# Graph network, last attention layer: normed rows gathered and multiplied by tile, exponentials ahead of the preceding step's normalization, heads mixed in one instruction

## The reference

```python
xt = jnp.matmul(x, weight).reshape(-1, heads, out_ch)
row, col = (edge_index[0], edge_index[1])
alpha_l = jnp.einsum('ehd,hd->eh', xt[row], attn_l)
alpha_r = jnp.einsum('ehd,hd->eh', xt[col], attn_r)
alpha = jax.nn.softmax(jax.nn.leaky_relu(alpha_l + alpha_r, 0.01), axis=1)
tmp = jnp.einsum('nh,nhd->nd', alpha[:n], xt[col[:n]])
out = jnp.broadcast_to(tmp[:, None, :], (n, heads, out_ch))
```

## Time and profile before

| | us |
|---|---|
| median of 3 runs | 3559.73 |
| lowest and highest run | 3539.03, 3561.72 |
| the profiled execution, its own time | 3567.03 |
| its span, first to last instruction | 3565.2 |
| TensorE busy (matmuls) | 2424.9 |
| VectorE busy | 2395.4 |
| ScalarE busy | 1352.5 |
| GpSimd busy | 1734.6 |

### The profile page before, as it was taken

The page is one execution under the profiler, slowest core; times in us unless marked ns, Lnnn a source line. Parts: engine busy times, 40 slices in busy tenths (PEclk is TensorE's granted clock), DMA queues, the critical chain, the costliest instruction groups (busy, mean ns, idle before and its releaser), DMA issues. The chain is left out here.

```text
span 3565.2 us, 41686 instructions
## 1 busy us (share of the span) xinstructions
PE 2424.9 (68%) x12339; PEld 1976.6 (55%) x12339; DVE 2395.4 (67%) x4693; ACT 1352.5 (38%) x2800; POOL 1734.6 (49%) x1269
## 2 busy tenths in 40 slices
PE   4668733454555543666621999879999999925998
PEld 3522213454444443444421897469888988923788
DVE  5979945777777778877886544344565566615788
ACT  2268833444444441000000435424434434423776
POOL 0257887776667667888888777730000000042000
PEclk9779865555555555888855999889999999966999
DMA  9993224665555656555533774146545645340355
GB/s 373 351 355 34 22 26 130 174 171 164 165 165 166 172 170 137 133 142 134 143 40 39 202 177 89 1 103 185 175 126 172 185 130 173 118 103 8 109 173 176
DMA packets 338453, 517.84 MB, mean 145 GB/s; under 512 B 145379, under 2 KB 227100, under 8 KB 331580
## 3 DMA queue, kind: packets, MB, share of 16 engines
q1 hardware_dynamic: 190254, 436.41, 38.2%
q0 software_dynamic: 134768, 58.41, 14.2%
q10 hardware_dynamic: 13214, 20.35, 1.7%
HBM read 369.65 MB, written 145.38 MB: 144 GB/s over the span
## 5 line engine op out<-in xcount | busy, mean ns | idle before, releaser
L1133 PE MATMUL banks<-rows_r,lhs_r 128*128 128x448 f32 x3500 | 899.1, 372 | 84.0 <-issue 41.6
L728 POOL DMA_INDIRECT counts<-wts x391 | 637.4, 1630 | 307.9 <-DMA counts<-ring 141.0
L1133 PEld LDWEIGHTS banks<-rows_r,lhs_r 128*128 128x128 f32 x3500 | 667.8, 191 | 152.9 <-issue 74.8
L741 POOL DMA_INDIRECT weights<-wts x391 | 620.9, 1588 | 161.8 <-issue 159.1
L1133 PE MATMUL banks<-ring_r,lhs_r 128*128 128x448 f32 x1750 | 525.8, 370 | 0.0
L749 POOL DMA_INDIRECT reg<-tab_p,w x416 | 406.9, 978 | 217.9 <-issue 122.8
L548 DVE SCALAR_TENSOR_TENSOR ring_r<-ring,dinv,rows_r 128x896 fp32r<-128x896 f32 (+1 forms) x300 | 303.7, 1033 | 309.5 <-ACT rows_r L535 309.3
L1221 PE MATMUL banks<-lhs_r,oT 128*128 x416 | 203.3, 489 | 429.8 <-issue 346.6
L535 ACT ACTIVATE rows_r<-ring,dinv 128x896 fp32r<-128x896 f32 (+1 forms) x300 | 285.0, 951 | 399.3 <-PE banks L1133 342.0
L799 POOL DMA_INDIRECT el<-tab_l,base_i x25 | 24.0, 958 | 796.8 <-DMA tab_l<-reg 789.5
L1221 PEld LDWEIGHTS banks<-lhs_r,oT 128*128 128x128 f32 x416 | 131.9, 317 | 447.3 <-issue 447.0
(11 more groups left out here) (269 smaller groups left out, 4104.6 us busy)
## 6 DMA issues: line engine op xcount, KB each, us to landing
ring<-weights SPq DMA_DIRECT2D x225, 448.0 KB
ring<-counts SPq DMA_DIRECT2D x150, 448.0 KB
zbuf<-reg SPq DMA_DIRECT2D x208, 256.0 KB
reg<-zbuf SPq DMA_DIRECT2D x52, 1024.0 KB
counts<-ring SPq DMA_DIRECT2D x25, 1568.0 KB, 16.4
weights<-ring SPq DMA_DIRECT2D x25, 1568.0 KB
ring<-weights SPq DMA_DIRECT2D x75, 224.0 KB
dr<-low_rows_d SPq DMA_DIRECT2D x52, 256.0 KB
```

Of the source, the lines that this page charges most:

```text
L728: pool.indirect_dma_start(counts, bass.IndirectOffsetOnAxis(ap=ix_c[:, k:k + 1], axis=0), vals_c[:, k:k + 1], None, compute_op=ALU.add).th ...
L741: pool.indirect_dma_start(weights, bass.IndirectOffsetOnAxis(ap=ix_w[:, k:k + 1], axis=0), vals_w[:, k:k + 1], None, compute_op=ALU.add).t ...
L1133: m = pe.matmul(bank[:, 0:BLK], lhs[part], rows[:, c:c + BLK], start=first, stop=last)
```

## The change

Four things are changed, all in the third layer and its mixing.

- tab_x holds the normed rows themselves (256 columns) and is stored from g_nat as soon as a step's five tiles are normed; tab_l is stored last. For it TensorE multiplies the transposed tiles by the 4 source columns alone, into one bank (stage "lg"), once all groups are transposed.
- GpSimd gathers the normed rows first (x_edge), and the small rows of step q behind the normed rows of step q+1.
- The product is done on the gathered rows, by tile, in each step: TensorE transposes a tile (stage "gx"), ScalarE copies it to one of two buffers (edge_T), TensorE multiplies by 260 columns (stage "xt"), ScalarE copies the result to xt_edge. ScalarE does this, and the exponential of the next step, right behind the square root of a step and ahead of the normed tiles of the step before it.
- The four heads are multiplied, and added to x_nat, in one instruction each.

The diff:

```diff
--- before.py
+++ after.py
@@ -132,6 +132,20 @@
     return unit_keys(gi, 0) + unit_keys(gi, 1)
 
 
+def rows_step(q):
+
+    ts = range(q * LG, (q + 1) * LG)
+    order = [(ts[0], "gx")]
+    for t in ts[1:]:
+        order += [(t, "gx"), (t - 1, "xt")]
+    return order + [(ts[-1], "xt")]
+
+
+def normed_groups(q):
+
+    return range(max(0, q - 3) * LG // 4, -(-NT // 4) if q == NSPLIT else max(0, q - 2) * LG // 4)
+
+
 def psum_plan():
 
     tg = [(j, g) for g in range(-(-NT // 4)) for j in range(JH)]
@@ -160,12 +174,12 @@
     for li in range(3):
         add(f"agg1{li}", dense, "V")
         add(f"cv{li}", pairs, "V")
-    for g in range(-(-NT // 4)):
-        add("gT2", [(j, g) for j in range(JH)], "A")
-        if g:
-            add("xt", [(t,) for t in range(4 * g - 4, 4 * g)], "A")
-    add("xt", [(t,) for t in range(NT - 1 - (NT - 1) % 4, NT)], "A")
-    add("gT3", tg, "A")
+    add("gT2", tg, "A")
+    add("lg", [(0,)], "A")
+    for q in range(NSPLIT + 1):
+        for t, stage in rows_step(q) if q < NSPLIT else ():
+            add(stage, [(t,)], "A")
+        add("gT3", [(j, g) for g in normed_groups(q) for j in range(JH)], "A")
     add("xj", pairs, "V")
     add("xi", [(j, b) for j in range(JH) for b in range(NB)], "A")
     add("a1", [(b,) for b in range(NB)], "A")
@@ -207,7 +221,7 @@
         zbuf = nc.dram_tensor("zbuf", (P, KS, H), F32).ap()
         cells = nc.dram_tensor("cells", (NCH, P), F32).ap()
         low_rows_d = nc.dram_tensor("low_rows_d", (KS, P), BF16).ap()
-        tab_x = nc.dram_tensor("tab_x", (NP, XE), F32).ap()
+        tab_x = nc.dram_tensor("tab_x", (NP, H), F32).ap()
         tab_l = nc.dram_tensor("tab_l", (NP, HEADS), F32).ap()
         counts_rows = counts[0:SPARE].rearrange("(r c) o -> r (c o)", c=LD)
         weights_rows = weights[0:SPARE].rearrange("(r c) o -> r (c o)", c=LD)
@@ -323,7 +337,7 @@
         supT, x0T, dinv_row = view(RD, JH, NP), view(RE, JH, NP), view(RF, DR)
 
         gT2 = view(RF, JH, NP)
-        xt_nat, xt_edge = view(RD, NT, XW), view(RD + NT * XW, NT, XE)
+        x_edge, lg_nat, xt_edge = view(RD, NT, H), view(RD + NT * H, NT, HEADS), view(RD + NT * XW, NT, XE)
         mix = view(RD, NT, H)
 
         xiT, xj_nat, a1row = view(RD, JH, NP), view(RE, NT, H), view(RF, LD)
@@ -352,6 +366,7 @@
         out_pair = [w2a_flat[:, BLK:BLK + 2 * H].rearrange("p (t c) -> p t c", c=H), w2b[:, 2:4, :]]
         attn = w1[:, 0:2, :]
         attn_tmp = w1[:, 2:4, :]
+        edge_T = [attn_tmp[:, k, :] for k in range(2)]
         ab2row, wa2row = w2b[:, 0, :], w2b[:, 1, :]
 
         def table(k):
@@ -682,11 +697,11 @@
                     sp.dma_start(attn[:, 1, :], attn_r.rearrange("h d -> (h d)").unsqueeze(0).to_broadcast([P, H])).then_inc(gat_loaded, 16)
 
             for s in range(NSPLIT):
-                sp.wait_ge(drained_a, nth[number["xt", ((s + 1) * LG - 1,)]])
-                if s == NSPLIT - 1:
-                    sp.dma_start(tab_l.rearrange("(t p) c -> p t c", p=P), xt_nat[:, :, XE:XW]).then_inc(l_stored, 16)
+                sp.wait_ge(ln_out, 2 * NT + (s + 1) * LG)
                 sp.dma_start(tab_x[s * LG * P:(s + 1) * LG * P].rearrange("(t p) c -> p t c", p=P),
-                             xt_nat[:, s * LG:(s + 1) * LG, 0:XE]).then_inc(xt_stored, 16)
+                             g_nat[:, s * LG:(s + 1) * LG, :]).then_inc(xt_stored, 16)
+            sp.wait_ge(drained_a, nth[number["lg", (0,)]])
+            sp.dma_start(tab_l.rearrange("(t p) c -> p t c", p=P), lg_nat).then_inc(l_stored, 16)
             sp.wait_ge(filled, number["h3", (JH - 1, NB - 1)] + 1)
             sp.dma_start(ab2row, ab2.unsqueeze(0).to_broadcast([P, H])).then_inc(gat_loaded, 16)
             sp.dma_start(wa2row, wa2.unsqueeze(0).to_broadcast([P, H])).then_inc(gat_loaded, 16)
@@ -793,16 +808,16 @@
                 pool.dma_start(ix[:, 0:NT - 1], dram[0:full].rearrange("(t p) -> p t", p=P)).then_inc(gi_ready, 16)
                 pool.dma_start(ix[0:LAST, NT - 1:NT], dram[full:N].unsqueeze(1)).then_inc(gi_ready, 16)
             pool.wait_ge(gi_ready, 64)
-            pool.wait_ge(l_stored, 16)
-            for s in range(NSPLIT):
-                for t in range(s * LG, (s + 1) * LG):
+            pool.wait_ge(xt_stored, 16 * NSPLIT)
+            for s in range(NSPLIT + 1):
+                for t in range(s * LG, (s + 1) * LG) if s < NSPLIT else ():
+                    pool.indirect_dma_start(x_edge[:, t, :], None, tab_x,
+                                            bass.IndirectOffsetOnAxis(ap=i_dst[:, t:t + 1], axis=0)).then_inc(edge_x[s], 16)
+                if s == 1:
+                    pool.wait_ge(l_stored, 16)
+                for t in range((s - 1) * LG, s * LG) if s else ():
                     pool.indirect_dma_start(el[:, t, :], None, tab_l,
-                                            bass.IndirectOffsetOnAxis(ap=i_src[:, t:t + 1], axis=0)).then_inc(edge_l[s], 16)
-                if s == 0:
-                    pool.wait_ge(xt_stored, 16 * NSPLIT)
-                for t in range(s * LG, (s + 1) * LG):
-                    pool.indirect_dma_start(xt_edge[:, t, :], None, tab_x,
-                                            bass.IndirectOffsetOnAxis(ap=i_dst[:, t:t + 1], axis=0)).then_inc(edge_x[s], 16)
+                                            bass.IndirectOffsetOnAxis(ap=i_src[:, t:t + 1], axis=0)).then_inc(edge_l[s - 1], 16)
 
             pool.wait_ge(ln_out, 4 * NT)
             pool.tensor_tensor(x_nat, x_nat, g_nat, ALU.add).then_inc(x_plus, 1)
@@ -833,29 +848,30 @@
                         for j in range(JH):
                             bank = empty_bank(act, number[stage, (j, g)])
                             emptied(act.activation(dest[:, j, ts[0] * P:(ts[-1] + 1) * P], bank[:, 0:len(ts) * P], ACT.Copy))
-                        if stage == "gT2" and g:
-                            copy_rows(g - 1)
                     copied[0] = upto
 
                 if stage == "hT":
                     act.wait_ge(drained_v, 3)
+                before(0)
                 for q in range(NT // LG):
-                    before(q)
                     act.wait_ge(ln_var, k * (NT // LG) + q + 1)
                     ts = slice(q * LG, (q + 1) * LG)
                     act.activation(sc[:, 1, ts], sc[:, 0, ts], ACT.Sqrt).then_inc(ln_std, 1)
+                    if q + 1 < NT // LG:
+                        before(q + 1)
                     if q:
                         apply(q - 1)
                 apply(NT // LG - 1)
                 if stage:
                     copy_groups(-(-NT // 4))
-                if stage == "gT2":
-                    copy_rows(-(-NT // 4) - 1)
-
-            def copy_rows(g):
-                for t in tiles_of((g,), 4):
-                    bank = empty_bank(act, number["xt", (t,)])
-                    emptied(act.activation(xt_nat[:, t, :], bank[:, 0:XW], ACT.Copy))
+
+            def copy_rows(q):
+                for t, stage in rows_step(q):
+                    bank = empty_bank(act, number[stage, (t,)])
+                    if stage == "gx":
+                        emptied(act.activation(edge_T[t % 2], bank[:, 0:H], ACT.Copy))
+                    else:
+                        emptied(act.activation(xt_edge[:, t, :], bank[:, 0:XE], ACT.Copy))
 
             def copy_pairs(stage, dest):
                 for g in range(-(-NT // 2)):
@@ -994,7 +1010,11 @@
 
             layernorm(2, stage="gT2", dest=gT2)
 
+            bank = empty_bank(act, number["lg", (0,)])
+            emptied(act.activation(lg_nat.rearrange("p t c -> p (t c)"), bank[:, 0:NT * HEADS], ACT.Copy))
+
             def exponentials(q):
+                copy_rows(q)
                 act.wait_ge(exp_in, q + 1)
                 ts = slice(q * LG, (q + 1) * LG)
                 act.activation(al[:, ts, :], al[:, ts, :], ACT.Exp).then_inc(exp_out, 1)
@@ -1040,9 +1060,9 @@
                     pe.wait_ge(drained[plan[prev_of[g]][2]], nth[prev_of[g]])
                 return ps[bank_of[g]]
 
-            def to_T(stage, src_nat, done, base, behind=None):
-
-                for gi in range(-(-NT // 4)):
+            def to_T(stage, src_nat, done, base, groups=range(-(-NT // 4))):
+
+                for gi in groups:
                     for j in range(JH):
                         bank = open_bank(number[stage, (j, gi)])
                         ts = tiles_of((gi,), 4)
@@ -1052,10 +1072,6 @@
                             m = pe.transpose(bank[:, (t - ts[0]) * P:(t - ts[0] + 1) * P],
                                              src_nat[:, t, j * P:(j + 1) * P], ident[:, :])
                         m.then_inc(filled, 1)
-                    if behind and gi:
-                        behind(gi - 1)
-                if behind:
-                    behind(gi)
 
             def node_rows(stage, lhs, rhs, width=H, per=2, nk=JH, base=0, block_ready=None):
 
@@ -1305,20 +1321,34 @@
 
             pe.wait_ge(gat_w_ready, 2 * JH)
 
-            def row_group(g):
-
```

(52 more changed lines are left out.)

## The result

The changed kernel takes 3573.42 us (median of 13 runs, 3561.93 to 3581.79) against 3558.73 us for the kernel before (13 runs, 3539.03 to 3566.52). The ratio is **1.0050, 95% interval 1.0033 to 1.0066**: half a per cent slower, 14.7 us by the medians, where no change (-0.3 us) was forecast. The profiled execution of after is its fastest, 3561.93 us with a span of 3560.2; that of before was 8 us above its median. The two spans therefore hide the loss, and the stretch from the third normalization's first square root (3103.29 before, 3092.61 after: 10.7 us earlier, in work that the change leaves alone) to x@W2 is the thing to compare.

A forecast was written before the change was run, and what follows sets the result against it. Bound mostly by TensorE in line 1133's dense products; the change shifts only x@W2's start. Start -6.5, steps +1.2, tail -4.0, waits +9 sum to -0.3 us: forecast 3559 us, range 3534 to 3583.

The forecast's parts named there:

- The start: Third layer's tables: small table ready when before, five gathers instead of ten ahead of first logits, 6.5 us saved.
- the row's price: TensorE's new row of 50 four-column matmuls, 100 records: 17.5 us at 1.2 GHz, 8.8 at 2.4, taken as 13.
- The steps of the loop: Four mixing steps between logits: 18.35 us each without waits, 73.4 against 72.2 before, +1.2 us.
- R: Per-step block of ScalarE copies, TensorE transposes and products ahead of next logits: 8.8 us; 6.1 warm, 11.1 cold throughout.
- the tail: Last logits to x@W2: 3.6 us less waiting for the exponential and 0.4 from merged heads, -4.0 us.
- rival (b): Copies of gathered rows serialize the loop at 1.2 GHz, R 11.1: +22.4 us, 3582 us; chance 0.17.
- rival (c): Mixing loop: products hidden and loop paced by gathers, 12.9 us a step: -31 us, 3528 us; chance 0.06.
- rival (a): Mixing loop: TensorE stays at 2.4 GHz, R 6.1, no waits, fast small matmuls: -24.3 us, 3535 us; chance 0.17.
- Merged heads: VectorE's mixing: one 1,280-column instruction of about 1.48 us replaces four taking 1.70; 0.2 saved twice, 0.4 a step.
- The waits: Mixing loop while gathers run: before holds 23.3 us of waits; the new loop's share taken as 9, ends 0 and 18.
- The two rules: VectorE-GpSimd port lock and hidden instruction fetch: waits term 2 to 4 us instead of 9; sum some 4 us lower.
- Rival (d): Small table ready 8 us late since stores, ring loads and row gathers share DMA engines: 3567 us; chance 0.15.

The follow-up runs named there:

- k11: Changed kernel with the row of small matmuls 16 columns wide instead of 4; executed once, the row took 21.49 us against 21.47.
- k1: Changed kernel with the small table's 4-column product made group by group behind the transposes; ratio to the kernel before 1.0023 (1.0007 to 1.0040).
- k15: The kernel before, unchanged, run again on a chip where it takes 3454 to 3461 us; ratio 1.0004 (0.9994 to 1.0014).
- k7: The kernel before with VectorE's mixing held until all fifty gathers have landed; one run, 3596.64 us.
- k10: The changed kernel with TensorE's work on gathered rows held until all fifty gathers have landed; one run, 3614.28 us.
- k4: The kernel before with only the four heads multiplied, and added to x_nat, in one instruction each; ratio 0.9965 (0.9949 to 0.9980).
- k13: The kernel before with the four heads multiplied in one instruction, the addition left in four; ratio 1.0006 (0.9994 to 1.0019).
- k14: The kernel before with the addition to x_nat's four heads in one instruction, the multiplication left in four; ratio 1.0005 (0.9995 to 1.0016).
- k17: The kernel before with exponentials ahead and merged heads, on a chip where before takes 3454 to 3461 us; ratio 0.9993 (0.9983 to 1.0003).
- k6: The kernel before with only exponentials ahead and merged heads, products left ahead of the tables; ratio 0.9947 (0.9932 to 0.9963), repeated 0.9952.
- k16: The changed kernel, run again on a chip where before takes 3454 to 3461 us; ratio to before 1.0048 (1.0032 to 1.0065).

## Why the prediction was wrong

**The start: the step that failed outright.** "So 17.5 us at 1.2 GHz and, halved, 8.8 us at 2.4 ... I take 13": the row took 21.47 us, above even the upper bound. The small table was stored 7.9 us later than before instead of at the same time, and the start became +2.1 us instead of -6.5. The rest of this term was right: the row began 27.1 us behind the square root, as forecast within half a us, and five gathers fewer saved 6.2 us, forecast 6.5.

Two errors lie in the row's price. The nearest row was chosen by columns (50 against 4), though k11 shows no difference between 4 and 16: each record of such a row waits for a weight load of 128x128. The price of that load stood among the rows, as eight loads in 1.66 us, 0.21 each, and was used only for transposes; times 100 it gives 20.8. The row that was chosen says the same once its loads are read. The 0.175 us run from the start of its first matmul to the start of the next line's; its four weight loads began at 860.90 and the next line's at 861.75, 0.21 us each. And the clock: TensorE never rose in this row, although it was busy through all of it, while it did rise in the products' block. This window of after shows it:

```profile
3120.40:3142.00 21.60, 21.60 (x102) 21.28 (x101) 0.00 (x0) 0.56 (x2) 9.68 (x10) 0.50 0.47 61
```

The Trainium skill, "TensorE: Matmul & The Clock Gate", section "LDWEIGHTS (loading the stationary operand)", gives a load's time as its columns divided by 1.2 in ns, 107 ns for 128. k1's 0.122 us at 2.4 GHz is near it, the 0.213 at 1.2 GHz twice as long; an estimate from that figure puts the row at 10.7 us, half of what it took.

In before TensorE went from transposes to products and back without a gap, and its granted clock was 1.00 from 3105 to 3142. In after it only transposed there, with gaps; the clock fell from 1.00 to 0.50 between 3111 and 3112, 8 us ahead of the row. In k1, with small groups between the transposes, it fell between 3116 and 3117. That the products which were taken away had kept it up is likely, but no run tests it alone.

**The steps of the loop held.** R was put at 8.8 and measured 8.0, a step at 18.35 and measured 17.1 to 17.2, the tail at -4.0 and measured -4.2. The clock rises inside each block, as argued from the earlier trace rows. Four steps were thus put 5.0 us too high (73.4 against 68.4), which happened to hide more than half of the error at the start. That the copies serialize the loop was in the forecast and in rival (b); the clock was the forecast's; rival (c), gather-paced, and rival (a), warm throughout, are both excluded. Merged heads took 1.49 us, forecast 1.48, and the wait for the exponential was 0.65 us.

**The waits: the second step that failed.** That before's 72.2 us held 23.3 us of waits was nearly right: without them the same four steps take 50.5 us (k15), 21.7 less. That they belong to gathers in flight is shown by k7 and k10. After's own share, put at 9 us, measured 11.9, 19.2 and (k11) 17.4. "About half of the new loop is TensorE's and ScalarE's, for which this stage shows no such waits" is the sentence that failed: in after all of them lie in just that half, and VectorE's mixing, which was to carry them, has none. In before TensorE stood idle for 66 us up to 3210.13, under the gathers, so that nothing of its could be held up. The two rules that the prediction set against its rows would both have made the term smaller; it came out larger.

With the sizes measured the sum for the first profile is start +2.1, steps 68.4 + 11.9 - 72.2 = +8.1, tail -4.2: +6.0, and for the second, with a start of +2.8, +14.0. The timed difference of 14.7 us is that of the second. So against the forecast of -0.3 the start is 9 us worse, the waits 3 to 10 us worse and the steps 5 us better. On a chip B neither side has waits and the loss is 21.7. The sum was a balance of four terms, and it came near zero only because two of them were put too low.

**What was not asked.** "0.2 saved, twice, 0.4 a step" priced the merged heads by busy time. Where the waits exist they are worth six times the 2 us of busy time (k4, -0.35% with interval 0.20 to 0.51, 12.5 us). On chips B, where gathers pace the steps, one merge alone gained nothing measurable (k13, k14), nor did both with the exponentials ahead (k17); k4 itself was not executed there. The changed kernel has the merged heads, and its mixing is free of those waits, but the block of products is not. Against k6 it is 1.0050 to 0.9947, about 1% behind: that is what storing normed rows and moving the products costs on chips A, and 0.55% on a chip B. In before the products lay beside copies and normalization, and the logits still came 2 us earlier than in after. The loss is that they moved from there into a loop that waits for them, with a hand-over for every tile.

**Rival (d)** named the late small table, 8 us, for another reason (contention of transfers). It was late by 7.9 us, by the matmuls; contention can have added the 0.9 us by which the store took longer to land, 9.1 against 8.2.

**What stays open.** The waits without releaser come with gathers in flight and only on some chips; what makes them there was not found. Nor is it known why merging the heads ends most of VectorE's, nor whether the number of instructions does it, since the test made for that met a chip without them. Nor is it known why the waits of ScalarE's and TensorE's block differ so from trace to trace.

## What to carry to other kernels

Price a row of narrow matmuls by its weight loads and not by its columns, and look up the granted clock that is left when the work around it has been taken away: here it was 1.00 before and 0.50 after. Before bringing a transfer forward, look for the last input of what it feeds: here ten gathers came 22 us earlier and waited for a table that came 8 us later. And when before's stage holds waits that the profile can't name, give two sums, with them and without, since another chip or another order of instructions may be free of them, and don't take an engine to be spared because it had nothing to do there.

## What the hardware showed

The same program differs by 3% between chips, and the place is the stretches with gathers: 88 us ahead of the third normalization and 25 in the stretch of the change, against 109 us between the two spans. VectorE's waits at line 1599, in the gathers of the first layers, in before on a chip A and then on a chip B:

```profile
DVE reg L1599 <- remote: 105.5, 28, 11.0
```

```profile
DVE reg L1599 <- DMA reg<-tab_p,w: 87.3, 26, 50.9
...
DVE reg L1599 <- PE banks L1221: 44.9, 34, 3.0
DVE reg L1599 <- issue: 30.3, 28, 4.5
```

The 105.5 us put down to "remote", up to 11.0 us each, have no counterpart on the chip B, where no wait of VectorE or ScalarE in the whole program is put down so; waits marked "issue" are there on both (26.1 us at this line on the chip A). All idle time ahead of the line is 264.0 us on the chip A and 163.3 on the chip B, and the third normalization is reached 88 us earlier there (3015.66 against 3103.29). GpSimd's issue of a gather is the same on both, 0.96 us and 0.30 between two. A few GpSimd gathers were longer: 2.26 us instead of 0.96 where VectorE multiplied the heads of its first step (3163.41 to 3164.90 above), and 2.20 us at the same place on the chip B (k16), where VectorE shows no wait beside it.

The Trainium skill, "SBUF — State Buffer", section "Who interferes with whom", would bound a mutual delay of VectorE and GpSimd by one instruction. The longer gathers fit that: 1.3 us more, beside an instruction of VectorE of 1.49 us. VectorE's waits of 5.9 and 11.0 us on chips A, and ScalarE's beside them (90.7 us "remote" at line 929, up to 10.6 each), do not, and the same instruction order without them on a chip B speaks against it as their cause.
